# Decoder layer, feed-forward: the quantised activations turned by a DMA instead of by TensorE and VectorE

## The chip, the cores and the metric

The kernel runs on one core of one Trainium2 chip. The metric is the device time of one execution in microseconds (us). Three executions of the kernel before were timed, and one more was recorded by the hardware profiler. Times in rows of the trace count from the start of the profiled span.

## The reference, cut to what matters

The layer has three parts, each added to x: an attention, a long convolution, and a feed-forward part. Only the last is touched. It works on 2048 rows (8 sequences of 256) of 512 numbers, with ternary weights and activations rounded to whole numbers between -127 and 127:

```python
def activation_quant(x):
    scale = 127.0 / jnp.clip(jnp.max(jnp.abs(x), axis=-1, keepdims=True), EPS, None)
    return jnp.clip(jnp.round(x * scale), -128.0, 127.0) / scale
def bit_linear(x, w):                       # w: weight_quant(w), ternary
    return jnp.einsum('bsh,oh->bso', activation_quant(x), weight_quant(w))

gate = bit_linear(x, w_gate)                # 512 -> 2048
up = bit_linear(x, w_up)                    # 512 -> 2048
activated = up * jnp.square(jax.nn.relu(gate))
activated = subln(activated, subln_weight)  # by the row's mean square, times a weight
return bit_linear(activated, w_down)        # 2048 -> 512
```

The last `bit_linear` sums over the 2048 columns of `activated`. TensorE sums over partitions, so the rounded activations, which lie with a row of the batch in each partition, have to be turned so that a column lies in each partition. The change is to how they are turned.

## The kernel before, in words

The work is cut into NT = 16 tiles of 128 rows. Each of the five queues (SyncE, TensorE, ScalarE, VectorE, GpSimd) runs its own list of instructions in order, and they meet at semaphores. In the feed-forward part, `schedule` (L966) calls each engine's `turn(t, r, ...)` for t = 0 to 15, turns 4 to 13 in a loop of two (r = t mod 2, the buffer). The order inside a turn is written out by hand. A turn works on three or four tiles at once: it makes the activations of tile t, ends the quantisation of tile t-1, does the down projection of tile t-2, and prepares the rows of tile t+2.

A tile's 2048 columns go through in four chunks of 512 (n = 0 to 3):

- TensorE (L1057): for each chunk 4 matmuls for the gate and 4 for up (L1066). After chunk 0 it turns the convolution's output of tile t+2 (L1027); after chunk 1 it turns the rounded activations of tile t-2, 16 blocks of 128x128 bf16, into PSUM (`turn_act`, L1043); after chunk 2 it turns the rows of tile t+1 (L1035). At the end of the turn come the 16 matmuls of the down projection of tile t-2 (`down`, L1054). The matmuls of chunks 2 and 3 wait for VectorE's chunks 0 and 1 to free their PSUM banks.
- ScalarE (L1114): relu (L1093) and square (L1095) of each gate chunk; the sum of squares of each product (L1104); the copy of the turned rows (L1108); and, between the sums of chunks 2 and 3, the scaling of all of tile t-1 (`quantise`, L1112).
- VectorE (L1235): the product of each chunk (`chunk`, L1189), the largest of each chunk (`greatest`, L1193), the scales of tile t-1 (`scale`, `scale_b`, L1199 to L1219), the layer norm and rounding of tile t+2 (`rows_x2` L1138, `rows_stats` L1143, `rows_mean` L1148, `rows_norm` L1156, `rows_greatest` L1160, `rows_scale`, `rows_int` L1175 to L1179). It copies the turned activations of tile t-2 out of PSUM in two halves (`act_out`, L1225): half 0 just before `scale_b`, whose first instruction (L1211) waits for GpSimd's power r4 (L1314), and half 1 just after chunk 2. The last instruction of a turn is `final` (L1233), which ends tile t-2.
- GpSimd (L1326): the weighing of each chunk (`weigh`, L1318), two small powers (L1314), and at the end of the turn the rounding of tile t-1 to bf16 (`integers`, L1324) into act8.
- SyncE: DMAs of the convolution's output into `conv_part` for the tile to be turned (`place`, L986), and the stores of finished tiles (`store`, L994).

Turns 0 and 1 have no down projection (`last=False`), so in them neither `turn_act`, `act_out`, `down` nor `final` is issued. Turns 14 and 15 prepare no more rows (`rows=False`). Behind turn 15 come the scales of tile 15, its quantisation and rounding, and then `turn_act`, both `act_out`, `down`, `final` and the store of tiles 14 and 15, one after the other.

Of the kernel before, what the change touches and what calls it, by code (L numbers as in the profile page):

```python
# [31 lines left out]
P = 128  # L32
# [35 lines left out]
def wait(eng, signal, turn, n):  # L68
    eng.wait_ge(signal.sem, signal.at(turn, n))  # L69


def apart(eng):

    eng.nop(nofuse=True)
# [824 lines left out]
def ffn(nc, ctx, m, g, out, multiply, add_up):  # L899
# [5 lines left out]
    def sb(name, shape, dt=F32):  # L905
        return ctx.enter_context(nc.sbuf_tensor(name, shape, dt))

    def two(name, shape, dt=F32):
        return [sb(f"{name}{r}", shape, dt) for r in range(2)]

    def sig(name, per=1):
        return Signal(ctx.enter_context(nc.semaphore("f_" + name)), per)
# [23 lines left out]
    act_w = [m.big[:, 0:FF], m.big[:, FF:2 * FF]]  # L936
    act32 = m.big[:, 2 * FF:3 * FF]
    act8 = [y.bitcast(BF16)[:, 0:FF] for y in ys]
    act8t = sb("act8t", [P, FK, P], BF16)
    mb4 = sb("mb4", [P, IC])  # L940
    cc, sm, var, r4, cr, mb, bm, rb, qs = (sb(n, [P, 1]) for n in (
        "cc", "sm", "var", "r4", "cr", "mb", "bm", "rb", "qs"))
    fd = two("fd", [P, 1])
    ot = two("ot", [P, C])
    GB, UB, TB, NB, DB = m.ps[:, 0:2, :], m.ps[:, 2:4, :], m.ps[:, 4, :], m.ps[:, 5:7, :], m.ps[:, 7, :]
    tbb = TB.bitcast(BF16)

    first_banks, first_rows = [GB[:, 0, :], GB[:, 1, :]], UB[:, 0, :].bitcast(BF16)
    nbb = NB.rearrange("p a b -> p (a b)").bitcast(BF16)

    d_g, c_ident, c_half, c_w3 = (sig(n) for n in ("g_in", "ident", "half", "w3"))
    s_turned, s_x2, s_bn, s_mv, s_ve, s_rs, s_xn = (sig(n) for n in (
# [3 lines left out]
    s_g, s_u, s_rl, s_r2, s_a, s_as, s_w, s_mb4 = (sig(n, IC) for n in ("g", "u", "rl", "r2", "a", "as", "w", "mb4"))  # L956
    s_sm, s_cc, s_var, s_r4, s_mb, s_cr, s_bm, s_rb, s_qs, s_fd = (sig(n) for n in (
        "sm", "cc", "var", "r4", "mb", "cr", "bm", "rb", "qs", "fd"))
    s_a32, s_a8, s_a8t, s_dn, s_fin = (sig(n) for n in ("a32", "a8", "a8t", "dn", "fin"))
    s_a8e = sig("a8e", 2)  # L960
    d_place = sig("d_place", 16)
    d_o = [sig("d_o0"), sig("d_o1")]

# [19 lines left out]
    def sync(sp):  # L983

        def place(t, half=0):
            sp.dma_start(conv_part[:], qo[:, :, bass.ds(t * T - half * (B * T - P), P)]).then_inc(d_place.sem, 16)  # L986

        def place_next(t, half=0):
            wait(sp, s_turned, t - 1, 1)
            place(t, half)  # L990

        def store(t, r, half=0):
            wait(sp, s_fin, t, 1)
            sp.dma_start(outv[bass.ds(t * TT - half * (NT - 1), 1)].rearrange("o p c -> (o p) c"), ot[r][:]  # L994
                         ).then_inc(d_o[r].sem, 16)

        sp.wait_ge(m.s_red.sem, H2 // 2)
        place(2)
        sp.wait_ge(m.s_tern.sem, PIECES)
        sp.dma_start(gb[:], g.rearrange("(o n) -> o n", o=1).broadcast_to([P, FF])).then_inc(d_g.sem, 16)  # L1000
        place_next(3)
        place_next(4)
        for t in range(3):
            place_next(t + 5)
            store(t, t % 2)
        sp.wait_ge(m.s_red.sem, H2)
        place_next(B, 1)
        store(3, 1)
        with sp.Fori(2, 4) as i:
            for r in range(2):  # L1010
                place_next(2 * i + r + 5, 1)
                store(2 * i + r, r)
        for t in range(B, B + 3):
            place_next(t + 5, 1)
            store(t, t % 2, 1)
        for t in range(B + 3, NT):
            store(t, t % 2, 1)
        for r in range(2):
            sp.wait_ge(d_o[r].sem, 16 * NT // 2)

    def tensor(pe):
# [13 lines left out]
                mm = pe.transpose(bank[:, k * P:(k + 1) * P], xq[r][:, k * P:(k + 1) * P], identb[:])  # L1035
            mm.then_inc(s_xqt.sem, 1)

        def turn_act(t, r, first=False):
            wait(pe, s_a8, t, 1)
            if not first:  # L1040
                wait(pe, s_a8e, t - 1, 2)
            for k in range(FK):
                mm = pe.transpose(nbb[:, k * P:(k + 1) * P], act8[r][:, k * P:(k + 1) * P], identb[:])  # L1043
            mm.then_inc(s_a8t.sem, 1)

        def down(t, first=False):
            if first:
                pe.wait_ge(m.s_tern.sem, PIECES)
            else:
                wait(pe, s_fin, t - 1, 1)  # L1050
            for k in range(FK):
                if k % (FK // 2) == 0:
                    wait(pe, s_a8e, t, k // (FK // 2) + 1)
                mm = pe.matmul(DB, act8t[:, k, :], down_w[:, k, :], start=(k == 0), stop=(k == FK - 1))  # L1054
            mm.then_inc(s_dn.sem, 1)

        def turn(t, r, after=True, last=True, rows=True, more=True, stored=True, pair=None):  # L1057
            wait(pe, s_xqe, t, 1)
            for n in range(IC):
                if n >= 2:  # L1060
                    wait(pe, s_a, t, n - 1)
                elif after:
                    wait(pe, s_a, t - 1, n + 3)
                for bank, wt, s in ((GB, gate_w, s_g), (UB, up_w, s_u)):
                    for k in range(CK):
                        mm = pe.matmul(bank[:, n % 2, :], xqt[r][:, k, :], wt[:, k, n * C:(n + 1) * C],  # L1066
                                       start=(k == 0), stop=(k == CK - 1))
                    mm.then_inc(s.sem, 1)
                if n == 0 and rows:
                    turn_conv_part(t + 2)  # L1070
                if n == 1 and last:
                    turn_act(t - 2, r, first=not stored and r == 0)
                if n == 2 and more:
                    turn_rows(t + 1, 1 - r, behind=rows)
            if last:
                down(t - 2, first=not stored and r == 0)

        pe.wait_ge(m.s_red.sem, H2 // 2)
        pe.wait_ge(m.s_z1.sem, H2 - 1)
# [4 lines left out]
        pe.wait_ge(m.s_tern.sem, PIECES * 2 // 3)  # L1084
        schedule(turn, pe.Fori)
        for t in (NT - 2, NT - 1):
            turn_act(t, t % 2)
            down(t)

    def scalar(act):  # L1090
        def relu(t, n):
# [40 lines left out]
    def vector(dve):  # L1132
# [86 lines left out]
            nc.vector.tensor_scalar(fd[r][:], bm[:], m.wmean[:, 2:3], 1.0 / 127.0, ALU.mult, ALU.mult  # L1219
                                    ).then_inc(s_fd.sem, 1)  # L1220

        def act_out(t, h):
            wait(dve, s_a8t, t, 1)
            half_k, half_n = FK // 2, FF // 2
            nc.vector.tensor_copy(act8t[:, h * half_k:(h + 1) * half_k, :].rearrange("p k t -> p (k t)"),  # L1225
                                  nbb[:, h * half_n:(h + 1) * half_n]).then_inc(s_a8e.sem, 1)

        def final(t, r, stores):
            wait(dve, s_dn, t, 1)
            wait(dve, s_fd, t, 1)  # L1230
# [4 lines left out]
        def turn(t, r, after=True, last=True, rows=True, more=True, stored=True, pair=None):  # L1235
# [15 lines left out]
                scale(t - 1, 1 - r)  # L1251
            if rows:
                rows_mean(t + 2)
            if last:
                act_out(t - 2, 0)
            if after:
                scale_b(t - 1, 1 - r)
            if rows:
                rows_var(t + 2)
            greatest(t, 0, r)  # L1260
            chunk(t, 2)
            if last:
                act_out(t - 2, 1)
            greatest(t, 1, r)
            if rows:
                rows_norm(t + 2)
# [37 lines left out]
        scale(NT - 1, 1)  # L1304
        scale_b(NT - 1, 1)
        for t in (NT - 2, NT - 1):
            for h in range(2):
                act_out(t, h)
            final(t, t % 2, NT // 2 - 1)

    def gpsimd(pool):
# [6 lines left out]
            nc.gpsimd.tensor_tensor(act_w[r][:, n * C:(n + 1) * C], a[n % 2][:], gb[:, n * C:(n + 1) * C], ALU.mult  # L1318
                                    ).then_inc(s_w.sem, 1)

        def integers(t, r):
            wait(pool, s_a32, t, 1)
            apart(pool)
            nc.gpsimd.tensor_scalar(act8[r][:], act32, 1.0, -MAGIC, ALU.mult, ALU.add).then_inc(s_a8.sem, 1)  # L1324

        def turn(t, r, after=True, last=True, rows=True, more=True, stored=True, pair=None):  # L1326
            weigh(t, 0, r)
            if after:
                power(r4, var, s_var, s_r4, t - 1)
            weigh(t, 1, r)  # L1330
            if rows:
                power(rs, ve, s_ve, s_rs, t + 2)
            weigh(t, 2, r)
            weigh(t, 3, r)
            if after:
                integers(t - 1, 1 - r)

        nc.gpsimd.memset(identb[:], 0.0).then_inc(c_ident.sem, 1)
        pool.wait_ge(c_ident.sem, 1)
# [103 lines left out]
```

## Time and profile before

| what | value |
|---|---|
| median of 3 executions | 687.07 us (686.49 to 687.9) |
| profiled execution, its time | 686.38 us |
| profiled execution, its span | 684.6 us |
| mean granted TensorE clock over the span | 0.970 |
| TensorE matmul busy | 624.9 us, 91% |
| VectorE busy | 508.5 us, 74% |
| ScalarE busy | 455.5 us, 67% |
| GpSimd busy | 269.7 us, 39% |
| VectorE, L1225, the 32 copies that the change takes out | 656 to 691 ns each |
| GpSimd, L1324, the 16 roundings | 1890 to 1915 ns each |

The span runs from the first to the last instruction; the execution's own time is 1.8 us longer. The feed-forward part takes about the last 225 us: turn 1 starts on VectorE at 475.9 us, turn 14 at 648.7 us. Shares of busy time are means over parts that are limited by different engines, so a stretch has to be read by itself. "Releaser" of a wait is the instruction whose end came last by the trace.

### The profile page before, as it was taken

How to read it: one execution, taken by the hardware profiler on the slowest of the kernel's cores; microseconds unless marked ns; L12 is line 12 of the kernel's file. 1: busy time of each engine (PE TensorE's matmuls, PEld its weight loads, DVE VectorE, ACT ScalarE, POOL GpSimd, SP SyncE). 2: the span in 40 equal slices, each digit the busy share in tenths (PEclk: the TensorE clock that was granted, in tenths of full speed). 3: DMA queues.
4: the chain of work that ended last, by engine and by line, in shares of the span. 5: the costliest groups of instructions: out<-in, count | busy, mean ns of one | idle time of the engine just before them, and what ended most of it. 6: DMA issues, size and time to landing. Idle time of an engine off the chain costs nothing.

```text
span 684.6 us, 10990 instructions
## 1 busy us (share of the span) xinstructions
PE 624.9 (91%) x3074; PEld 355.3 (52%) x3074; DVE 508.5 (74%) x981; ACT 455.5 (67%) x799; POOL 269.7 (39%) x248
## 2 busy tenths in 40 slices
PE   5889999999999998989999999948799999999995
PEld 3535454545454543467777777723344444444442
DVE  3556757575847373547887788789999999999983
ACT  2354666676665746168889888845876777577691
POOL 1000010001010003057777777624665666566572
PEclk9969999999999997999999999978999999999999
DMA  8564153627180816045666556511011100100001
GB/s 316 140 182 93 31 124 123 148 97 191 55 240 17 234 37 153 11 145 162 168 192 173 173 164 193 156 70 31 17 32 48 45 31 31 61 31 31 31 17 46
DMA packets 42309, 72.51 MB, mean 106 GB/s; under 512 B 4720, under 2 KB 16496, under 8 KB 42160
## 3 DMA queue, kind: packets, MB, share of 16 engines
q1 hardware_dynamic: 42288, 72.26, 36.7%
q8 instruction: 10, 0.16, 0.1%
q14 instruction: 11, 0.09, 0.0%
HBM read 47.51 MB, written 4.28 MB: 76 GB/s over the span
## 4 chain that ended last, share of the span: by engine, by line
PE 26%; DVE 24%; issue 5%; DVEq 1%; ACT 1%; POOL 0%; ACTq 0%; POOLq 0%
PE ps L708 20%; DVE toep L1189 4%; DVE xq L1175 3%; PE ps L1066 3%; DVE mb L1193 3%; DVE act8t L1225 2%; PE ps L1054 2%; DVE mx L1160 1%; DVE x_all L1138 1%; DVE st L1143 1%; DVE xn L1156 1%; DVE qo L761 1%; DVEq L69 1%; DVE ot L1233 1%; DVE cx L1171 0%
## 5 line engine op out<-in xcount | busy, mean ns | idle before, releaser
L708 PE MATMUL ps<-kv,toep 128*128 128x288 f32 x640 | 157.1, 409 | 1.1 <-PEq L1378 1.1
L708 PEld LDWEIGHTS ps<-kv,toep 128*128 128x128 f32 x640 | 122.2, 191 | 36.0 <-issue 2.2
L1066 PE MATMUL ps<-wt,xqt 128*128 128x512 bf16 x512 | 123.8, 387 | 9.4 <-DVE toep L1189 8.5
L1318 POOL TENSOR_TENSOR big<-toep,wst 128x512 f32<-128x512 f32 x64 | 83.6, 1306 | 59.7 <-DVE toep L1189 59.7
L396 ACT ACTIVATE big<-ps,kscale 128x512 f32<-128x512 f32 x128 | 84.3, 695 | 14.1 <-PE ps L246 13.3
L246 PE MATMUL ps<-qx,kx 128*128 128x512 f32 x128 | 76.7, 634 | 12.4 <-ACT big L396 12.1
L1066 PEld LDWEIGHTS ps<-wt,xqt 128*128 128x128 bf16 x512 | 48.3, 99 | 67.1 <-DVE toep L1189 11.9
L761 DVE TENSOR_REDUCE qo<-big 128x2048 f32 (+1 forms) x32 | 72.2, 2257 | 0.0
L1104 ACT ACTIVATE asq<-toep 128x512 f32<-128x512 f32 x64 | 39.5, 618 | 44.7 <-DVE sm L1199 43.7
L696 POOL TENSOR_TENSOR kv<-ctx 128x768 f32<-128x768 f32 (+1 forms) x32 | 52.5, 1642 | 37.0 <-PE ps L708 28.2
L750 DVE TENSOR_TENSOR big<-ps,qd 128x1024 f32<-128x1024 f32 x32 | 39.2, 1225 | 37.0 <-ACT ys L840 34.4
L1054 PE MATMUL ps<-wt,act8t 128*128 128x512 bf16 x256 | 59.9, 379 | 7.3 <-DVE act8t L1225 7.3
L550 DVE RECIPROCAL yt<-ps 128x512 f32<-128x512 f32 x16 | 53.6, 3351 | 14.6 <-PE ps L264 14.6
L217 PE MATMUL ps<-wq_s,xt 128*128 128x512 f32 x128 | 63.3, 593 | 0.8 <-ACT xt L360 0.8
L800 POOL TENSOR_TENSOR big<-ys,qd 128x768 f32<-128x768 f32 x32 | 56.3, 1759 | 13.7 <-ACT ys L840 11.5
L284 PE MATMUL ps<-wo_s,yt 128*128 128x512 f32 x128 | 56.6, 594 | 1.0 <-DVE yt L555 1.0
L246 PEld LDWEIGHTS ps<-qx,kx 128*128 128x128 f32 x128 | 25.7, 205 | 46.4 <-ACT big L396 26.6
L646 POOL COPY vo<-vn 128x256 f32<-128x256 f32 x8 | 3.2, 397 | 111.7 <-PE ps L273 86.3
L1189 DVE TENSOR_TENSOR toep<-ps,kv 128x512 f32<-128x512 f32 x64 | 43.5, 680 | 3.8 <-ACT kv L1095 2.4
L1054 PEld LDWEIGHTS ps<-wt,act8t 128*128 128x128 bf16 x256 | 23.9, 98 | 40.4 <-DVE act8t L1225 11.0
L1093 ACT ACTIVATE kv<-ps 128x512 f32<-128x512 f32 x64 | 37.6, 587 | 10.6 <-PE ps L1066 10.6
L1193 DVE TENSOR_REDUCE mb<-big 128x1 f32<-128x512 f32 x64 | 43.3, 677 | 0.0
(121 smaller groups left out, 1018.5 us busy)
## 6 DMA issues: line engine op xcount, KB each, us to landing
qx<-kv SPq DMA_DIRECT2D x128, 128.0 KB, 2.4
wst<-in_wall SPq DMA_DIRECT2D x12, 1024.0 KB, 6.8
wst<-in_wall SPq DMA_DIRECT2D x48, 256.0 KB, 3.8
toep<-krows SPq DMA_DIRECT2D x32, 256.0 KB, 3.7
ctx<-in_ctxt SPq DMA_DIRECT2D x32, 192.0 KB, 2.6
out_y<-ot SPq DMA_DIRECT2D x16, 256.0 KB, 2.0
conv_part<-qo SPq DMA_DIRECT2D x14, 256.0 KB, 2.7
x_all<-in_x SPq DMA_DIRECT2D x2, 1536.0 KB, 14.4
```

Source lines behind the costliest of these rows:

```text
L217: mm = pe.matmul(bank[:, t, :], xt[:, k, t * P:(t + 1) * P], wq_s[:, k, :], start=(k == 0), stop=(k == CK - 1))
L246: pe.matmul(SB[:, n % 2, :], kx[:, kv, s * P:(s + 1) * P].bitcast(F32R), qx[:, kv, gp * C:(gp + 1) * C].bitcast(F32R), start=True, stop=Tr ...
L284: mm = pe.matmul(OB[:, t, :], yt[:, k, t * P:(t + 1) * P], wo_s[:, k, :], start=(k == 0), stop=(k == CK - 1))
L396: act.activation(pt[:, s, kv, gp * C:(gp + 1) * C], SB[:, n % 2, :], ACT.Exp, scale=kscale[:, c:c + 1]).then_inc(s_e.sem, 1)
L708: mm = pe.matmul(m.ps[:, LB * r + lb, :].rearrange("p (b s) -> p b s", s=WIDE)[:, :, 0:PAIRS], m.toep[r][:, d * P:(d + 1) * P], m.kv[r][:, ...
L761: nc.vector.tensor_reduce(qo[:, :, bass.ds(h * HD, HD)], z[r][:], AX.X, ALU.add).then_inc(s_red.sem, 1)
L800: nc.gpsimd.tensor_tensor(z[r][:, :, :, HD - SHIFTS:HD].rearrange("p n j s -> p n s j"), window(ys[r][:], SHIFTS - 1, (SHIFTS * EW, NB), ( ...
L1054: mm = pe.matmul(DB, act8t[:, k, :], down_w[:, k, :], start=(k == 0), stop=(k == FK - 1))
L1066: mm = pe.matmul(bank[:, n % 2, :], xqt[r][:, k, :], wt[:, k, n * C:(n + 1) * C], start=(k == 0), stop=(k == CK - 1))
L1189: nc.vector.tensor_tensor(a[n % 2][:], UB[:, n % 2, :], r2[n % 2][:], ALU.mult).then_inc(s_a.sem, 1)
L1193: nc.vector.tensor_reduce(mb4[:, n:n + 1], act_w[r][:, n * C:(n + 1) * C], AX.X, ALU.max, apply_absolute_value=True).then_inc(s_mb4.sem, 1)
L1318: nc.gpsimd.tensor_tensor(act_w[r][:, n * C:(n + 1) * C], a[n % 2][:], gb[:, n * C:(n + 1) * C], ALU.mult).then_inc(s_w.sem, 1)
```

## The change

`turn_act` of TensorE and `act_out` of VectorE are taken out. SyncE gets a `turn_act`: it waits for GpSimd's rounding of the tile and issues one DMA that reads act8 (128 partitions by 2048 bf16, 512 KB) and writes it turned into act8t (128 by 16 by 128). act8t is held twice, one buffer for even and one for odd tiles. TensorE's `down` waits for this DMA. GpSimd's `integers` of tile t newly waits for the down projection of tile t-2, which shows that the DMA has read act8's buffer. The PSUM banks that held the turned activations are no longer used.

```diff
-    act8t = sb("act8t", [P, FK, P], BF16)
+    act8t = two("act8t", [P, FK, P], BF16)
...
+        def turn_act(t, r):
+            wait(sp, s_a8, t, 1)
+            apart(sp)
+            sp.dma_start(act8t[r][:], act8[r], transpose=True).then_inc(d_a8t[r].sem, 16)
...
         place_next(4)
+        turn_act(0, 0)
         for t in range(3):
             place_next(t + 5)
+            turn_act(t + 1, (t + 1) % 2)
             store(t, t % 2)
         sp.wait_ge(m.s_red.sem, H2)
         place_next(B, 1)
+        turn_act(4, 0)
         store(3, 1)
         with sp.Fori(2, 4) as i:
             for r in range(2):
                 place_next(2 * i + r + 5, 1)
+                turn_act(2 * i + r + 1, 1 - r)
                 store(2 * i + r, r)
         for t in range(B, B + 3):
             place_next(t + 5, 1)
+            turn_act(t + 1, (t + 1) % 2)
             store(t, t % 2, 1)
-        for t in range(B + 3, NT):
+        for t in range(B + 3, NT - 1):
+            turn_act(t + 1, (t + 1) % 2)
             store(t, t % 2, 1)
+        store(NT - 1, 1, 1)
...
-        def turn_act(t, r, first=False):
-            wait(pe, s_a8, t, 1)
-            if not first:
-                wait(pe, s_a8e, t - 1, 2)
-            for k in range(FK):
-                mm = pe.transpose(nbb[:, k * P:(k + 1) * P], act8[r][:, k * P:(k + 1) * P], identb[:])
-            mm.then_inc(s_a8t.sem, 1)
-
-        def down(t, first=False):
+        def down(t, r, turned, first=False):
+            pe.wait_ge(d_a8t[r].sem, turned * 16)
             if first:
                 pe.wait_ge(m.s_tern.sem, PIECES)
             else:
                 wait(pe, s_fin, t - 1, 1)
             for k in range(FK):
-                if k % (FK // 2) == 0:
-                    wait(pe, s_a8e, t, k // (FK // 2) + 1)
-                mm = pe.matmul(DB, act8t[:, k, :], down_w[:, k, :], start=(k == 0), stop=(k == FK - 1))
+                mm = pe.matmul(DB, act8t[r][:, k, :], down_w[:, k, :], start=(k == 0), stop=(k == FK - 1))
...
-                if n == 1 and last:
-                    turn_act(t - 2, r, first=not stored and r == 0)
...
         for t in (NT - 2, NT - 1):
-            turn_act(t, t % 2)
-            down(t)
+            down(t, t % 2, NT // 2)
...
-        def act_out(t, h):
-            wait(dve, s_a8t, t, 1)
-            half_k, half_n = FK // 2, FF // 2
-            nc.vector.tensor_copy(act8t[:, h * half_k:(h + 1) * half_k, :].rearrange("p k t -> p (k t)"),
-                                  nbb[:, h * half_n:(h + 1) * half_n]).then_inc(s_a8e.sem, 1)
...
-            if last:
-                act_out(t - 2, 0)
             if after:
                 scale_b(t - 1, 1 - r)
...
             chunk(t, 2)
-            if last:
-                act_out(t - 2, 1)
             greatest(t, 1, r)
...
         for t in (NT - 2, NT - 1):
-            for h in range(2):
-                act_out(t, h)
             final(t, t % 2, NT // 2 - 1)
...
-        def integers(t, r):
+        def integers(t, r, after=True):
             wait(pool, s_a32, t, 1)
+            if after:
+                wait(pool, s_dn, t - 2, 1)
             apart(pool)
```

## Rows read from the trace of the kernel before

**Rows 1.** Windows of a middle turn and of turn 1: length, busy by engine, clock, DMA.

```profile
core 0: us, PE busy (x) PEld busy (x) DVE busy (x) ACT busy (x) POOL busy (x), PEclk, DMA share, GB/s
581.99:595.33 13.34, 12.42 (x75) 6.19 (x73) 13.06 (x35) 9.59 (x19) 8.14 (x7) 1.00 0.12 39
475.86:488.55 12.69, 9.28 (x54) 4.32 (x53) 11.90 (x32) 10.31 (x20) 8.14 (x7) 1.00 0.15 43
```

**Rows 2.** Timeline of the middle turn: start, us, engine, line, operation, [idle before <-releaser].

```profile
581.99 0.68 DVE L1189 TENSOR_TENSOR toep<-ps,kv 128x512 f32<-128x512 f32 x1
...
585.55 0.66 DVE L1225 COPY act8t<-ps 128x1024 bf16<-128x1024 bf16 x1
585.56 0.55 POOL L1314 TENSOR_TENSOR r<-var,fhalf 128x1 f32<-128x1 f32 x1 [1.51 <-DVE var L1204]
...
586.14 0.21 DVE L1211 TENSOR_SCALAR cr<-r,cf_all 128x1 f32<-128x1 f32 x1
...
587.82 0.68 DVE L1189 TENSOR_TENSOR toep<-ps,kv 128x512 f32<-128x512 f32 x1
...
588.41 0.68 DVE L1225 COPY act8t<-ps 128x1024 bf16<-128x1024 bf16 x1
588.58 1.30 POOL L1318 TENSOR_TENSOR big<-toep,wst 128x512 f32<-128x512 f32 x1 [0.64 <-DVE toep L1189]
...
589.61 0.56 DVE L1156 TENSOR_SCALAR xn<-x_all,mv,rs 128x512 f32 x1
...
590.08 0.68 DVE L1189 TENSOR_TENSOR toep<-ps,kv 128x512 f32<-128x512 f32 x1
```

**Rows 3.** Timeline of turn 1, which has no L1225.

```profile
475.86 0.68 DVE L1189 TENSOR_TENSOR toep<-ps,kv 128x512 f32<-128x512 f32 x1
...
479.44 0.55 POOL L1314 TENSOR_TENSOR r<-var,fhalf 128x1 f32<-128x1 f32 x1 [1.52 <-DVE var L1204]
...
480.02 0.21 DVE L1211 TENSOR_SCALAR cr<-r,cf_all 128x1 f32<-128x1 f32 x1 [0.51 <-POOL r L1314]
...
482.45 1.29 POOL L1318 TENSOR_TENSOR big<-toep,wst 128x512 f32<-128x512 f32 x1 [0.64 <-DVE toep L1189]
...
482.88 1.15 DVE L1156 TENSOR_SCALAR xn<-x_all,mv,rs 128x512 f32<-128x512 f32 x1
...
483.95 0.68 DVE L1189 TENSOR_TENSOR toep<-ps,kv 128x512 f32<-128x512 f32 x1
```

**Rows 4.** DMA issues: transfer, count, KB each, median us from issue to landing.

```profile
out_y<-ot SPq DMA_DIRECT2D x16, 256.0 KB, 2.0
conv_part<-qo SPq DMA_DIRECT2D x14, 256.0 KB, 2.7
...
wst<-in_g SPq DMA_DIRECT2D x1, 1024.0 KB, 4.6
```

**Rows 5.** Timeline, from one middle turn's chunk 0 on TensorE to the next down projection.

```profile
590.89 1.89 PE L1066 MATMUL ps<-wt,xqt 128*128 128x512 bf16 x8
...
592.11 1.90 POOL L1324 TENSOR_SCALAR ys<-big 128x2048 bf16<-128x2048 f32 x1
...
593.07 0.63 ACT L1095 ACTIVATE kv<-kv 128x512 f32<-128x512 f32 x1
...
600.18 1.89 PE L1054 MATMUL ps<-wt,act8t 128*128 128x512 bf16 x8
```

**Rows 6.** Timeline of the end: tiles 13 and 15.

```profile
657.61 1.90 POOL L1324 TENSOR_SCALAR ys<-big 128x2048 bf16<-128x2048 f32 x1 [0.49 <-ACT big L1112]
...
664.37 3.62 PE L1054 MATMUL ps<-wt,act8t 128*128 128x512 bf16 x16
...
668.02 0.75 DVE L1233 SCALAR_TENSOR_TENSOR ot<-ps,fd,x_all 128x512 f32<-128x512 f32 x1 [0.91 <-PE ps L1054]
...
673.73 1.90 POOL L1324 TENSOR_SCALAR ys<-big 128x2048 bf16<-128x2048 f32 x1 [3.30 <-ACT big L1112]
...
677.69 3.61 PE L1054 MATMUL ps<-wt,act8t 128*128 128x512 bf16 x16 [0.87 <-DVE act8t L1225]
```

**Rows 7.** Window after TensorE's idle stretch before turn 0: length, PE busy, clock, DMA.

```profile
457.00:462.40 5.40, 4.63 (x16) 0.50 0.05 21
```

More of the change, by code:

```diff
@@ L944, in ffn @@
     ot = two("ot", [P, C])
-    GB, UB, TB, NB, DB = m.ps[:, 0:2, :], m.ps[:, 2:4, :], m.ps[:, 4, :], m.ps[:, 5:7, :], m.ps[:, 7, :]
+    GB, UB, TB, DB = m.ps[:, 0:2, :], m.ps[:, 2:4, :], m.ps[:, 4, :], m.ps[:, 7, :]
     tbb = TB.bitcast(BF16)
     first_banks, first_rows = [GB[:, 0, :], GB[:, 1, :]], UB[:, 0, :].bitcast(BF16)
-    nbb = NB.rearrange("p a b -> p (a b)").bitcast(BF16)
     d_g, c_ident, c_half, c_w3 = (sig(n) for n in ("g_in", "ident", "half", "w3"))
@@ L958, in ffn @@
         "sm", "cc", "var", "r4", "mb", "cr", "bm", "rb", "qs", "fd"))
-    s_a32, s_a8, s_a8t, s_dn, s_fin = (sig(n) for n in ("a32", "a8", "a8t", "dn", "fin"))
-    s_a8e = sig("a8e", 2)
+    s_a32, s_a8, s_dn, s_fin = (sig(n) for n in ("a32", "a8", "dn", "fin"))
+    d_a8t = [sig("d_a8t0"), sig("d_a8t1")]
     d_place = sig("d_place", 16)
@@ L1075, in turn @@
             if last:
-                down(t - 2, first=not stored and r == 0)
+                down(t - 2, r, pair if stored else 1, first=not stored and r == 0)
         pe.wait_ge(m.s_red.sem, H2 // 2)
@@ L1335, in turn @@
             if after:
-                integers(t - 1, 1 - r)
+                integers(t - 1, 1 - r, after=last and (stored or r == 1))
         nc.gpsimd.memset(identb[:], 0.0).then_inc(c_ident.sem, 1)
```

## The prediction

> **What bounds the kernel now.** The change touches only the feed-forward turns, so I read stretches, not the page's totals. First the windows of one turn in the middle: 13.34 us long, VectorE busy 13.06 us of it and TensorE 12.42 us [rows 1]. Both look full, and a reader would subtract here: two copies less on VectorE, 16 block transposes less on TensorE, a shorter turn. The window cannot say that; it counts an instruction as busy also where it is held up. So I next put two timelines side by side: the middle turn [rows 2], and turn 1, which has no down projection yet and so neither copy [rows 3]. Turn 1 is a trial of the change's effect on VectorE that the kernel before already holds. From its first product (chunk 0) to L1211, the first instruction that needs GpSimd's power, the middle turn takes 586.14 - 581.99 = 4.15 us and turn 1 480.02 - 475.86 = 4.16 us. From L1211 to chunk 3 it is 590.08 - 586.14 = 3.94 us with the copy and 483.95 - 480.02 = 3.93 us without. Turn 1 is 12.69 us against 13.34 [rows 1], and the 0.65 us between them is `final`, which turn 1 lacks too (0.75 us a piece [rows 6], each instruction starting a little before the end of the one before). The two copies lie in time that VectorE would otherwise wait out.
>
> **Part 1, the copies (L1225).** Half 0 runs 585.55 to 586.21 beside GpSimd's power, which starts at 585.56 and ends at 586.11; L1211 starts at 586.14 [rows 2]. Without the copy L1211 waits for the same power: in turn 1 it stood idle 0.51 us, released by L1314 [rows 3]. Worth nothing. The cover is the power and the scales before it, and those stay. Half 1 starts at 588.41 and pushes what follows by 0.60 us, so that L1156 starts at 589.61 and takes 0.56 us. GpSimd's weighing L1318 runs from 588.58 to 589.88 [rows 2]. Without the copy L1156 would start at 589.01, inside that. In turn 1 it does: it starts at 482.88 while L1318 runs from 482.45 to 483.74, and takes 1.15 us instead of 0.56, to end 0.29 us behind L1318's end [rows 3]; in the middle turn it ends at 590.17, also 0.29 us behind L1318's end. So half 1 is worth nothing either: VectorE is held up by GpSimd instead. Sum for the 12 turns 2 to 13: 0 us, with 0.59 us each (7.1 us) as the other bound of one half, 14.2 us of both. I take 0, because turn 1 measures it.
>
> **Part 2, the transposes on TensorE (L1043).** They stand between chunk 1 and chunk 2. Chunk 2's matmuls wait for VectorE's chunk 0, chunk 3's for its chunk 1, and VectorE's order is unmoved by part 1. TensorE idles a little more; nothing on the path gets earlier. 0 us. At the end, turn 15 has less to do on VectorE and TensorE, but tile 13's down projection will wait for its DMA there (part 4), so I take 0 again; the bound below is -0.6 us, the place of one copy on VectorE.
>
> **Part 3, the DMA.** No row shows a transposing DMA. What is needed is L, from the end of the rounding to the turned tile in SBUF. SyncE is idle when the rounding ends (the store of the tile before waits for `final`, later; the placing has been issued a turn ago), so L is issue to landing. By bytes: 256 KB land in 2.0 us and 1024 KB in 4.6 us [rows 4], so 512 KB in about 2.9 us. That is the lower bound. By pieces: `conv_part` has the bytes of `out_y` in 512 pieces (4 rows of 512 B for each partition) instead of 128 and takes 0.7 us longer [rows 4], 1.8 ns for each piece more. A turned 128x128 block of bf16 has rows of 256 B, 2048 of them in the tile: 2.9 + 1920 x 1.8 ns = 6.4 us. The upper bound is everything by pieces, four times `conv_part`: 10.8 us. I take 6.4 us, since the cost of pieces is measured on a copy inside SBUF like this one. The trace shows no transfer at all in which data are turned, so nothing here tells how much slower or not that is. The Trainium skill, Advanced Engine Details and Errata, section on the X-bar transpose, says that such a DMA is as fast as a regular one; by it L would be the 2.9 us of the byte rows.
>
> Is L covered in a middle turn? The rounding ends at 592.11 + 1.90 = 594.01 and the down projection of that tile starts at 600.18 [rows 5]: 6.17 us. If it starts later, the next chunk 0 on TensorE is late, then its relu and square, then VectorE's chunk 0. From that chunk 0 on TensorE (590.89) to the end of its square (593.07 + 0.63) are 2.81 us [rows 5]; VectorE takes the product at 595.33, the end of the window [rows 1], 1.6 us later. TensorE also loses 0.42 us in `down` now, waiting for half 1, which goes. So L up to 8.2 us costs a middle turn nothing. Beyond that the loop is: VectorE's chunk 0 to the rounding's end 594.01 - 581.99 = 12.02, then L, then `down` 3.62 [rows 6], then 2.81, over two turns: 18.45 + L against 2 x 13.34 = 26.68. With L = 6.4: 0 us. SyncE's stores and placings come behind the transpose in its queue by its issue time; they are needed a turn later and cost nothing. GpSimd's new wait, `integers` on the down projection two tiles back, is met by then (that projection ended before 590.89, the rounding starts at 592.11 [rows 5]), and only the next turn's weighing stands behind it. 0 us.
>
> **Part 4, the end.** Here the cover is gone. Tile 13 is rounded at 657.61 + 1.90 = 659.51; its down projection started at 664.37 [rows 6], 4.86 us later, and now starts L later. `final` of tile 13 (668.02) follows it, and on VectorE the last largest value and all scales of tile 15 stand behind `final`; the rounding of tile 15 (673.73) follows these. First term: L - 4.86. Then tile 15 is rounded at 675.63 and was projected at 677.69 [rows 6]: 2.06 us for transposes, copies and all. Second term: L - 2.06. With L = 6.4: 1.5 + 4.3 = 5.9 us. Only the store is behind it, as before. TensorE's clock: after its idle stretch before turn 0 the window shows a granted clock of 0.50, that is 1.2 GHz, for about 5 us [rows 7]. At the end TensorE now idles for over 5 us between the projections of tiles 13 and 14. At the upper level a matmul of `down` takes 3.62 / 16 = 0.23 us [rows 6]; at half the clock half of tile 14's 16 would cost some 1.8 us more, but the wait for tile 15's own DMA covers most of that. I take 0, bound +1.8.
>
> **The sum:** 0 + 0 + 0 + 5.9 = +5.9 us on the profiled execution (686.38 us; its span 684.6 and 1.8 around it), which stands 0.7 us below the median of 687.07. I add it to the median: 693.0 us. A measurement of this kernel can tell about 0.2% (1.4 us) from no change.
>
> **The rivals.**
>
> *A, the forecast, 46%.* L between 4.1 and 8.2 us: only the end pays, twice. The first term starts from 0 at L = 4.86, so +2.0 to +9.5 us: 689 to 696.6 us.
>
> *B, the DMA is quick, 15%.* L from 2.9 to 4.1 us, the byte rows. Then the first term is 0 or a little below and the second 0.8 to 2.0: 687.3 to 689 us, mostly within 0.2%. Against it: the pieces of 256 B. The skill's rule named above is this case.
>
> *C, late by pieces, 22%.* L over 8.2 us, up to the 10.8 of the rows and somewhat past. At 10.8 two turns take 29.25 us instead of 26.68, +2.6 us for each of 6 pairs = 15.4 us, and the end 2 x 10.8 - 6.92 = 14.7 us: 717 us. VectorE would then wait at chunk 0 (L1189) for ScalarE or TensorE every turn, where it has no idle time now. For it: cost by pieces, unknown cost of turning. Against: pieces overlapped well in `conv_part`.
>
> *D, faster, 10%.* The place is VectorE between chunk 2 and chunk 3 and at L1211. If L1156 were not held up by L1318 but ran in 0.56 us, and the power came earlier, turns 2 to 13 would each lose 1.19 us: -14.2 + 5.9 = -8.3, 678.8 us. Half 1 alone gives 7.1 us, -1.2 net, the point from which it decides. For it: VectorE is 98% busy by the window, and it loses two instructions. Against it: turn 1.
>
> *E, block by block, 7%.* The DMA turns 16 blocks of 128x128 one after the other. If each cost as much as the shortest row, 2.0 us [rows 4], L is 32 us, two turns take 50.5 us, +23.8 for each pair = 143, and the end +57: 887 us. The Trainium skill, Vector Engine: DVE Perf Modes, section on the three transpose paths, gives 1309 ns for a 128x128 block by DMA; by it, an estimate, 16 blocks in series are 21 us and the kernel near 800 us.
>
> **How the numbers follow.** The likeliest is A, at 693.0 us. 686.5 to 718 us holds A, B and 19 of the 22% of C; D and E and the rest of C, 20%, lie outside. A's own range is 689 to 697. Faster by over 0.2%: D, 10%. Within 0.2%: most of B, 14%. Slower: 76%.
>
> **What would show it.** The turns of the loop still 13.3 us; no L1225 and no L1043; L1211 idle 0.5 us before it, released by L1314, in every turn; L1156 at 1.15 us in all middle turns; the transposing DMA near 6.4 us to landing; TensorE waiting for DMA at L1054 for tiles 13, 14 and 15, and not before; the span from `final` of tile 13 to the end longer by 4.3 us. The forecast is wrong if the middle turn changes: shorter means D, longer with VectorE idle before chunk 0 means C or E. If the turn holds and the total is off, L was.

## The result, and the profile after

| | before | after |
|---|---|---|
| median | 686.58 us (6 executions) | 691.36 us (6 executions, 690.06 to 692.86) |
| ratio | | 1.0070, 95% interval 1.0053 to 1.0088 |
| span of the profiled execution | 684.6 us | 689.0 us |
| VectorE's chunk 0 of turn 0 | at 461.9 us | at 460.9 us |

The change costs 4.8 us; 5.9 were forecast. What comes ahead of the feed-forward part is untouched, but the start of turn 0 lies anywhere from 460.9 to 464.1 us in the profiled executions of the kernels shown here, one execution each. So from here on I compare stretches between the starts of chunk 0 on VectorE, each from one profiled execution, and set totals beside them.

First the middle turn, as in [rows 1]. It is 13.40 us long; TensorE has 1.05 us less to do and VectorE 0.45 us less, and neither shortens the turn:

```profile
581.40:594.80 13.40, 11.37 (x56) 5.32 (x56) 12.61 (x33) 9.48 (x18) 8.17 (x7) 1.00 0.33 78
```

The timeline of this turn shows why. It answers to [rows 2], line numbers moved by one (L1210 for L1211, L1155 for L1156, L1188 for L1189):

```profile
581.40 0.68 DVE L1188 TENSOR_TENSOR toep<-ps,kv 128x512 f32<-128x512 f32 x1
...
584.98 0.55 POOL L1301 TENSOR_TENSOR r<-var,fhalf 128x1 f32<-128x1 f32 x1 [1.51 <-DVE var L1203]
...
585.56 0.21 DVE L1210 TENSOR_SCALAR cr<-r,cf_all 128x1 f32<-128x1 f32 x1 [0.51 <-POOL r L1301]
...
587.99 1.31 POOL L1305 TENSOR_TENSOR big<-toep,wst 128x512 f32<-128x512 f32 x1 [0.64 <-DVE toep L1188]
...
588.42 1.16 DVE L1155 TENSOR_SCALAR xn<-x_all,mv,rs 128x512 f32 x1
...
589.50 0.68 DVE L1188 TENSOR_TENSOR toep<-ps,kv 128x512 f32<-128x512 f32 x1
```

L1210 now stands idle 0.51 us for GpSimd's power, where the first copy ran. L1155 takes 1.16 us instead of 0.56: it starts while GpSimd's weighing holds it up and ends 0.28 us behind that. Both are turn 1 of the kernel before [rows 3], to 0.01 us. Of the 1.34 us that the two copies took, nothing comes back.

The DMA, from issue to landing, as the last part of the profile's page has it:

```profile
act8t<-ys SPq DMA_TRANSPOSE x16, 4.3
```

4.3 us, against 6.4 forecast; a tile's down projection in a middle turn starts when it did.

The end, answering to [rows 6]:

```profile
668.40 0.75 DVE L1226 SCALAR_TENSOR_TENSOR ot<-ps,fd,x_all 128x512 f32<-128x512 f32 x1 [0.29 <-PE ps L1056]
...
674.94 1.90 POOL L1313 TENSOR_SCALAR ys<-big 128x2048 bf16<-128x2048 f32 x1 [3.33 <-ACT big L1111]
...
675.50 5.68 PE L1056 MATMUL ps<-wt,act8t 128*128 128x512 bf16 x16 [7.13 <-DMA act8t<-ys]
...
681.21 0.75 DVE L1226 SCALAR_TENSOR_TENSOR ot<-ps,fd,x_all 128x512 f32<-128x512 f32 x1 [8.46 <-PE ps L1056]
...
682.11 3.61 PE L1056 MATMUL ps<-wt,act8t 128*128 128x512 bf16 x16 [0.94 <-DVE ot L1226]
```

Tile 15 is rounded at 676.84 and projected at 682.11, 5.27 us later instead of 2.06. TensorE waited 7.13 us for tile 14's DMA, and then did that tile's 16 matmuls in 5.68 us instead of 3.62. The `final` of tile 14 came late by this, and tile 15's projection waited for it, 0.94 us beyond its own DMA. From the start of tile 13's `final` to the end of the span are 20.6 us instead of 16.6: 4.0 more, where 4.3 were forecast.

A place that the forecast did not have is in turn 14: chunk 2's 8 matmuls take 3.50 us, where they took 1.90. The windows of 3.5 us from there (PE busy, clock, DMA), first after, then the same place before:

```profile
649.09:652.59 3.50, 3.50 (x11) 0.53 0.79 185
```

```profile
649.43:652.93 3.50, 3.50 (x20) 1.00 0.19 75
```

The granted clock is 0.53 there, close to its lower level (1.2 GHz). TensorE had stood idle for 2.21 us, where in the kernel before the block transposes ran.

The same happens once more in the changed kernel, in turn 2, and there it costs nothing:

```profile
488.50 3.58 PE L1068 MATMUL ps<-wt,xqt 128*128 128x512 bf16 x8 [2.69 <-DVE toep L1188]
```

The granted clock over turn 2 is 0.87, as it is over turn 14 (0.86); before, both had 1.00. But turn 2 takes 13.34 us as before, because VectorE, and not TensorE, sets its pace. In turn 14, which has no rows to prepare and is 2.8 us shorter, TensorE's loss shows.

The account of the 5.4 us from chunk 0 of turn 0 to the end (before 222.7 us, after 228.1):

| stretch | before | after | difference |
|---|---|---|---|
| turns 0 and 1 | 26.67 | 26.86 | +0.2 |
| turns 2 to 13, each | 13.345 | 13.383 | +0.04, x12 = +0.5 |
| turn 14 | 10.55 | 11.83 | +1.3 |
| from chunk 0 of turn 15 | 25.36 | 28.81 | +3.4 |

The 0.2 us of turns 0 and 1 say little: in the kernels shown here this stretch takes 26.45 to 26.90 us.

### The profile page after: what moved, and what is told of

It is laid out like the page before. It is cut to its first block, busy times and chain, and to the rows that moved or that the text cites. A ratio compares the mean times of both kernels' runs of the same rounds, so it can differ in the third digit from the quotient of the medians.

```text
span 689.0 us, 10465 instructions
## 1 busy us (share of the span) xinstructions
PE 613.6 (89%) x2818; PEld 341.5 (50%) x2818; DVE 498.1 (72%) x949; ACT 455.0 (66%) x799; POOL 270.0 (39%) x248
## 4 chain that ended last, share of the span: by engine, by line
PE 25%; DVE 19%; issue 6%; POOL 3%; ACT 2%; DVEq 1%; DMA 1%; ACTq 0%; POOLq 0%; SPq 0%
PE ps L708 20%; DVE xq L1174 3%; DVE toep L1188 3%; PE ps L1068 3%; DVE mb L1192 3%; DVE xn L1155 2%; POOL big L1305 2%; PE ps L1056 2%; DVE mx L1159 1%; DVE qo L761 1%; POOL r L1301 1%; DMA act8t<-ys 1%; DVE ot L1226 1%; DVEq L69 0%; DVE cx L1170 0%
## 5 line engine op out<-in xcount | busy, mean ns | idle before, releaser
L1068 PE MATMUL ps<-wt,xqt 128*128 128x512 bf16 x512 | 126.9, 395 | 28.8 <-DVE toep L1188 28.0
L396 ACT ACTIVATE big<-ps,kscale 128x512 f32<-128x512 f32 x128 | 84.9, 695 | 13.7 <-PE ps L246 12.0
L800 POOL TENSOR_TENSOR big<-ys,qd 128x768 f32<-128x768 f32 x32 | 56.3, 1760 | 13.7 <-ACT ys L840 11.6
L1188 DVE TENSOR_TENSOR toep<-ps,kv 128x512 f32<-128x512 f32 x64 | 43.4, 679 | 4.8 <-ACT kv L1094 3.5
L1056 PEld LDWEIGHTS ps<-wt,act8t 128*128 128x128 bf16 x256 | 25.4, 100 | 40.3 <-DMA act8t<-ys 9.0
```

Of the source, the lines that this page charges most:

```text
L396: act.activation(pt[:, s, kv, gp * C:(gp + 1) * C], SB[:, n % 2, :], ACT.Exp, scale=kscale[:, c:c + 1]).then_inc(s_e.sem, 1)
L800: nc.gpsimd.tensor_tensor(z[r][:, :, :, HD - SHIFTS:HD].rearrange("p n j s -> p n s j"), window(ys[r][:], SHIFTS - 1, (SHIFTS * EW, NB), ( ...
L1056: mm = pe.matmul(DB, act8t[r][:, k, :], down_w[:, k, :], start=(k == 0), stop=(k == FK - 1))
L1188: nc.vector.tensor_tensor(a[n % 2][:], UB[:, n % 2, :], r2[n % 2][:], ALU.mult).then_inc(s_a.sem, 1)
```

## The experiments

**1. The block transposes back on TensorE, for nothing (warm).** They run where they did, also ahead of the last two down projections, and write PSUM that nobody reads; the DMA still feeds `down`.

```diff
+        def keep_warm(t, r):
+            wait(pe, s_a8, t, 1)
+            for k in range(FK):
+                pe.transpose(nbb[:, k * P:(k + 1) * P], act8[r][:, k * P:(k + 1) * P], identb[:])
...
+                if n == 1 and last:
+                    keep_warm(t - 2, r)
...
         for t in (NT - 2, NT - 1):
+            keep_warm(t, t % 2)
             down(t, t % 2, NT // 2)
```

> The changed kernel with TensorE's 16 block transposes of the old kernel put back at their old places, into PSUM banks that nobody reads (added work, the DMA still feeds the down projection). Theory 1 (the missing transposes let TensorE's clock fall at a few places: chunk 2 of turn 14 takes 3.50 us for 8 matmuls instead of 1.90, tile 14's down projection 5.68 instead of 3.62): both are back at 1.9 and 3.6 us, the kernel is 1.5 to 2.2 us faster than the changed one, about 689.3 us, although it does more work. Rival (the clock falls because of the waits for the DMA at the end alone): turn 14 is back, tile 14's down projection still takes over 5 us, and only 1.3 us return. Rival 2 (TensorE's work is on the path): slower than the changed kernel by up to 0.5 us a turn. The middle turn stays at 13.3 to 13.4 us in theory 1.

Median 691.04 us, ratio to before 1.0056 (1.0036 to 1.0077). Against the changed kernel's 691.36 us the executions show no gain. In the profiled one the start of turn 0 was at 463.6 us, 2.7 us later than in the changed kernel's; whether the edit itself moves that start was not tried. By stretches: turns 13.386 us, turn 14 10.55 (after: 11.83), from turn 15 on 27.94 (28.81); from turn 0, 225.6 against 228.1. Turn 14 is fully back, by added work. Tile 14's projection still takes 5.15 us: theory 1 is half wrong, the first rival holds for that place. That TensorE's work is on the path of the turn is refuted: the turns hold with the transposes in.

```profile
651.45 1.90 PE L1074 MATMUL ps<-wt,xqt 128*128 128x512 bf16 x8 [0.93 <-DVE toep L1197]
...
676.25 5.15 PE L1062 MATMUL ps<-wt,act8t 128*128 128x512 bf16 x16 [3.27 <-DMA act8t<-ys]
```

**2. Tiles 14 and 15 turned as before, the rest by DMA (tail).**

```diff
         for t in (NT - 2, NT - 1):
-            down(t, t % 2, NT // 2)
+            end_act(t, t % 2)
+            end_down(t, t % 2)
...
         for t in (NT - 2, NT - 1):
+            for h in range(2):
+                end_out(t, h)
             final(t, t % 2, NT // 2 - 1)
```

`end_act` is the 16 transposes into PSUM, `end_out` one of VectorE's two copies out of it, `end_down` the 16 matmuls behind them; SyncE issues no DMA for these two tiles.

> The changed kernel, but the last two tiles (14 and 15), whose turning nothing covers, are turned as before, by TensorE and VectorE's copies; tiles 0 to 13 by the DMA. Theory (the loss sits in the uncovered DMA waits of the last two tiles, 2.4 us, and in the clock that falls while TensorE waits there, 0.8 us): 3 to 3.5 us faster than the changed kernel, 688 us, ratio to the kernel before about 1.002, what is left being the slower chunk 2 of turn 14 (1.3 us). Rival (the loss is spread over the loop, contention of the 512 KB transfers with all engines): the end gives back under 1 us and the total stays above 690.

Median 689.75 us (ratio 1.0029, 1.0006 to 1.0052). The end: 26.99 us, 1.8 us back; turn 14 stays at 11.87. Less than the 3 us expected, since tile 14's projection still ran at a lowered clock, 4.98 us, though nothing waited for a DMA there. That is the profiled execution, the slowest of 12. Four of the 12 took 686.3 to 686.9 us at a mean granted clock of 0.967 or 0.968, as fast as the kernel before; the other eight took 689.3 to 692.5 us at 0.962 to 0.965, the profiled one among them (0.962). So the same kernel loses the clock in one execution and seems to keep it in another, and the stretches of one execution do not tell how often.

**3. Both (tail_warm).**

> The changed kernel with both earlier repairs: tiles 14 and 15 turned by TensorE and VectorE, and in the turns TensorE's 16 block transposes put back for nothing. Measured apart, from chunk 0 of turn 0 to the end: 222.7 us in the kernel before, 228.1 in the changed one, 225.6 with the transposes back, 226.3 with the end back. Theory (the loss is the uncovered DMA at the end and TensorE's lower clock in turn 14 and at tile 14's down projection, and nothing else): together 223.2 us or less, the 0.5 us left being the 12 turns at 13.38 instead of 13.34 us; ratio to the kernel before 1.000 to 1.003. Rival (something in the loop or in SyncE's queue costs as well): over 224.5 us.

Median 687.27 us, ratio 0.9991 (0.9973 to 1.0008). Turn 14 10.55, end 25.35, from turn 0 223.26 us; tile 14's projection is at 3.61 us:

```profile
673.12 3.61 PE L1070 MATMUL ps<-wt,act8t 128*128 128x512 bf16 x16 [1.36 <-DVE act8t L1251]
```

All 12 executions had a mean granted clock of 0.969 or 0.970. The two repairs together bring back all but 0.5 us, and this 0.5 is the 12 turns at 13.386 instead of 13.345. Here VectorE does only 4 of the 32 copies and TensorE all of the transposes: 28 copies less are worth nothing in this order of instructions.

**4. The copy's worth in another order (order_after, order_before).** In both kernels VectorE does the largest value of chunk 0 ahead of the scales, and the norm directly behind chunk 2.

```diff
             if after:
+                wait(dve, s_mb, t - 1, 1)
+            greatest(t, 0, r)
+            if after:
                 scale_b(t - 1, 1 - r)
             if rows:
                 rows_var(t + 2)
-            greatest(t, 0, r)
             chunk(t, 2)
-            greatest(t, 1, r)
             if rows:
                 rows_norm(t + 2)
+            greatest(t, 1, r)
```

In the kernel before, the norm also goes ahead of the second copy.

> The changed kernel with two instructions of VectorE moved: the largest value of chunk 0 goes ahead of the scales (into the wait for GpSimd's power), the layer norm of the next rows goes directly behind chunk 2 (ahead of GpSimd's weighing of chunk 2). Theory (the two copies that were taken out are worth 0.51 and 0.6 us a turn, hidden by two stalls: L1210 waiting for the power and the norm held up by the weighing): with the stalls filled the middle turn drops from 13.4 to 12.3 to 12.5 us, 12 turns bring 11 to 13 us, about 679 us, faster than both kernels. If only one stall goes, 12.9 us and 685 us. Rival (TensorE or ScalarE bounds the turn at 13.3 us as well): the turn stays above 13.2 us and the total within 1 us of 691.

> The kernel before, with the same two moves on VectorE and the two copies kept. Theory (in the kernel before both stalls were already filled, by the copies): the moves bring nothing, middle turn 13.2 to 13.4 us, total within 1.4 us of 686.6. Rival (the order alone is better, whatever the copies do): the turn falls as in the changed kernel with the moves, to 12.5 us, and the total to 675 us.

Both forecasts missed, and the pair says more than either. The changed kernel: 691.21 us (ratio 1.0068, 1.0045 to 1.0091), turn 13.34 us, no gain. The kernel before: 702.32 us (ratio 1.0220, 1.0195 to 1.0245), turn 14.58 us. In the same order the two copies cost 14.58 - 13.34 = 1.24 us a turn. The first stall was filled (L1210 waits no longer). The second grew, as the rows of the changed kernel in this order show:

```profile
586.85 1.68 DVE L1155 TENSOR_SCALAR xn<-x_all,mv,rs 128x512 f32 x1
...
586.95 1.30 POOL L1307 TENSOR_TENSOR big<-toep,wst 128x512 f32<-128x512 f32 x1
```

By the record the norm starts 0.10 us ahead of the weighing and still loses: it ends 0.28 us behind it. So it goes in 10 of the 12 turns (1.58 to 1.68 us). In turns 5 and 7 the norm went first and took 0.54 and 0.55 us, once with the same lead of 0.10 us. These two turns took 13.02 us, and not the 12.3 to 12.5 expected, for VectorE now met the next of GpSimd's instructions, the rounding (L1315, 538.23 to 540.20):

```profile
538.49 2.00 DVE L1178 TENSOR_SCALAR xq<-xq 128x512 bf16<-128x512 f32 x1
```

This took 0.42 us in the other ten. So what the first stall gave, the second took, and behind the second stands a third; with the copies in, nothing hides them any more. This bears out the reading of turn 1: the copies are real work that was free only where they stood.

**5. The DMA as a plain copy (plain),** which leaves the turning out, so that the down projection gets unturned activations.

```diff
-            sp.dma_start(act8t[r][:], act8[r], transpose=True).then_inc(d_a8t[r].sem, 16)
+            sp.dma_start(act8t[r].rearrange("p k t -> p (k t)"), act8[r]).then_inc(d_a8t[r].sem, 16)
```

> The changed kernel with the DMA of the activations as a plain copy of the same 512 KB between the same buffers (128 rows of 4 KB each, nothing is turned, so the down projection gets the activations unturned). It measures the cost of turning. Theory 1 (turning costs by its 256 B pieces or by the turning itself): the plain copy lands in about 2.9 us, against 4.3 us, its issue takes 0.3 to 0.4 us against 1.8. Rival (a transposing DMA is as fast as a regular one): the plain copy takes 4.0 to 4.3 us as well.

```profile
L999 SPq DMA_DIRECT2D act8t<-ys x16: 470/494/501, 488.8 to 678.8; - x16
...
DMA to landing us min/median/max: 2.9/2.9/3.3
```

Theory 1 holds. Issue 0.49 us (after: 1.80), landing 2.9 us (4.3). Turning costs 1.4 us of latency and 1.3 us of SyncE. Whether it does so by its 256 B pieces or by the turning itself, the plain copy, which has neither, cannot tell. The middle turn is 13.39 us here too: the DMA's cost inside is covered, whatever its form. Total 692.09 us in one execution, from turn 0 227.5 us, 0.6 less than the changed kernel, because the end waits 1.4 us less for a DMA but pays more of it to the clock (tile 14's projection 6.07 us).

**6. Three transposing DMAs for one (three_dma):** two more into free memory, ahead of the real one. SyncE waits in addition for the three of the tile before, which had landed long since in the rows below.

```diff
...
+                sp.wait_ge(d_a8t[1 - r].sem, before * 48)
             apart(sp)
+            for n in range(2):
+                sp.dma_start(spare[n], act8[r], transpose=True).then_inc(d_a8t[r].sem, 16)
             sp.dma_start(act8t[r][:], act8[r], transpose=True).then_inc(d_a8t[r].sem, 16)
...
-            pe.wait_ge(d_a8t[r].sem, turned * 16)
+            pe.wait_ge(d_a8t[r].sem, turned * 48)
```

> The changed kernel with two more transposing DMAs of the same tile, into memory that nobody reads, ahead of the real one; the down projection waits for all three (added work: 1 MB more to move for each tile). From rounding to landing 4.3 us become about 4.3 + 2 x 1.8 = 8 us, if the DMAs follow one another at the pace of the issues. Theory (up to 8.2 us are covered in a middle turn): the turn stays at 13.4 to 13.5 us, and what is lost lies behind chunk 0 of turn 14, 2 x 3.7 us or somewhat more. Rival (the cover is only the 6.2 us to the down projection, as TensorE has no slack behind it): each turn grows by about (8 - 6.2) = 1.8 us or half of that, 10 to 20 us for the loop. If the landing comes out at 9 us or more the theory says (18.45 + L) / 2 for a turn.

712.80 us in one execution. The issues took longer than I had taken, 2.3 us each; a middle turn of this kernel, from the rounding to `down`'s next wait:

```profile
586.56 1.90 POOL L1321 TENSOR_SCALAR ys<-big 128x2048 bf16<-128x2048 f32 x1
...
588.63 4.64 SPq L1006 DMA_TRANSPOSE big<-ys  x2
...
593.32 2.34 SPq L1007 DMA_TRANSPOSE act8t<-ys  x1
...
597.92 2.33 PE L1064 MATMUL ps<-wt,act8t 128*128 128x512 bf16 x10 [2.38 <-DMA act8t<-ys]
```

Rounded at 588.46, projected at 597.92: L = 9.5 us. The formula says (18.45 + 9.5) / 2 = 13.97 us for a turn; the mean of the 12 is 14.15. Ten of them lie between 13.4 and 14.2 us; turns 2 and 4 took 16.2 and 16.6 us, which the formula does not explain. TensorE's clock has a part in them: the granted clock was 0.79 and 0.90 over these two and 1.00 over the other ten, and the down projection, 3.62 us elsewhere, took 5.02 and 5.31 us in them. L was 9.4 to 10.4 us over the 12 turns, 9.7 in the mean, which gives 14.06. The rival (every microsecond beyond 6.2 counts, in full or by half) would give 16.7 or 15.0 us for a turn, and ten of the twelve lie well under both: there is slack behind the down projection.

**7. An order that uses the time (norm_final), and the same with the copies (norm_final_before).** The norm goes directly ahead of chunk 2; `final` goes ahead of the rounding on VectorE.

```diff
+            if after:
+                wait(dve, s_mb, t - 1, 1)
+            greatest(t, 0, r)
             if after:
                 scale_b(t - 1, 1 - r)
             if rows:
                 rows_var(t + 2)
-            greatest(t, 0, r)
+            if rows:
+                rows_norm(t + 2)
             chunk(t, 2)
             greatest(t, 1, r)
-            if rows:
-                rows_norm(t + 2)
             chunk(t, 3)
...
-            if rows:
-                rows_int(t + 2, r)
             if last:
                 final(t - 2, r, pair - 1 if stored else None)
+            if rows:
+                rows_int(t + 2, r)
```

> The changed kernel with three moves on VectorE: the largest value of chunk 0 ahead of the scales; the layer norm directly ahead of chunk 2, where GpSimd cannot start a weighing (it waits for chunk 2); the final of tile t-2 ahead of the rounding of tile t+2, into the time in which GpSimd's rounding holds VectorE's up. Theory (VectorE's turn is its instructions plus what GpSimd holds up, and TensorE and ScalarE have over 1 us to spare): the norm takes 0.5 to 0.6 us instead of 1.15 to 1.7, the held part of the rounding shrinks from 1.1 to 0.5 us, the turn drops from 13.4 to 12.5 to 13.0 us, 5 to 10 us less in all, 681 to 686 us. Rival (something else, ScalarE's chain or the down projection, bounds the turn at 13.3 us): no change, 691 us.

> The kernel before with the same three moves, copies kept. Theory (with VectorE's stalls filled otherwise, the two copies cost their 0.6 us each): the turn is 1.1 to 1.3 us longer than that of the changed kernel with the same moves, 13.7 to 14.2 us, total 690 to 697. Rival (the copies are free in any order): the same turn as there.

The changed kernel in this order: 684.48 us, ratio to the kernel before 0.9962 (0.9947 to 0.9978), turn 12.88 us. The kernel before in this order: 690.29 us, ratio 1.0045 (1.0023 to 1.0067), turn 13.61 us; a little under the 13.7 to 14.2 expected, and the difference of the two is under the 1.1 to 1.3 expected. The norm runs free now, since GpSimd has nothing that it could start before chunk 2:

```profile
584.63 0.55 DVE L1155 TENSOR_SCALAR xn<-x_all,mv,rs 128x512 f32 x1 [0.67 <-POOL rs L1303]
```

The rounding of the rows (L1174) is still held up, though: it takes about 1.48 us here, 1.72 in the changed kernel, 0.48 where nothing holds it up; less of that went than expected. The copies cost 13.61 - 12.88 = 0.73 us a turn in this order, between the 0 of the given order and the 1.24 of experiment 4.

**8. The version that beats both (best_tail), and with the spare transposes (best_tail_warm).** Experiment 7's order with experiment 2's end; then also experiment 1.

> The changed kernel with the three moves on VectorE that brought its turn from 13.38 to 12.88 us, and with tiles 14 and 15 turned by TensorE and VectorE as before. Theory: the stretch behind chunk 0 of turn 15 falls from 29.1 to about 27 us as it did alone (28.8 to 27.0), so 1.8 to 2.5 us less, 682.3 us in all, ratio to the kernel before 0.993. Rival (with the shorter turns the end is bound otherwise, by ScalarE): no gain over 684.5 us.

> The same as the kernel before it in this call, with the 16 block transposes back in TensorE's turns for nothing. Theory (they hold the clock at its upper level at the end, and TensorE has the time): 0.5 to 1.5 us less again, 681 us. Rival (with turns of 12.9 us TensorE's time is on the path): 1 to 5 us more, turns of 13.0 us and over.

best_tail: 682.22 us, ratio 0.9927 (0.9902 to 0.9952), turn 12.89, end 25.28 us: 5.4 us under the 687.64 us of the kernel before in the same series, and the theory held. best_tail_warm: 682.36 us (0.9928, 0.9903 to 0.9952), turns 12.89, but an end of 27.03 us, where tile 14's projection took 5.24 us at a lowered clock in spite of the transposes; in best_tail it took 3.61 without them. In the medians neither the gain of the theory nor the loss of the rival came. The two profiled executions differ by 2.2 us from chunk 0 of turn 0 to the end (219.1 against 216.9), which turn 0's earlier start (460.9 against 462.9) hides in the total; since the medians agree, I lay nothing on that difference.

## Why the prediction was right

*Parts 1 and 2, the loop is worth nothing: right, and shown.* The rows after repeat turn 1 of before [rows 3]. Experiment 3 takes 28 copies away and stands at the old time; experiment 4 shows the same copies at 1.24 us a turn once the order is another. What was not foreseen is +0.04 us a turn: L1174, the rounding of the rows, takes 1.70 to 1.74 us in turns 4 to 13 instead of 1.67. It ends 0.28 us behind GpSimd's rounding before and after, and that rounding starts 0.03 to 0.07 us later there, 10.16 to 10.19 us behind chunk 0 instead of 10.12 to 10.13. The change gave it a new wait, for the down projection two tiles back, and part 3 put that at 0 us. The shift is in experiments 1 to 3 and 5 alike, so it is neither TensorE's idling nor the turning. That the wait itself is the cause is likely, but no run takes it out.

*Part 3, L: the size was off.* Taken 6.4 us, measured 4.3, which is only just inside the 4.1 to 8.2 us of rival A. The number of pieces was right: the page counts 38000 packets under 512 B after and 4720 before, some 2080 a tile. So was the base, the plain copy's 2.9 us. Laid on the pieces alone, the price of one was 1.4 us / 1920 = 0.7 ns, not the 1.8 ns taken from `conv_part`. That 1.8 ns came from comparing `conv_part`, a copy inside SBUF, with `out_y`, a store to HBM, so its 0.7 us need not be the pieces' alone. The Trainium skill's rule, that a transposing DMA is as fast as a regular one (Advanced Engine Details and Errata, X-bar transpose), does not hold for this size: 4.3 us against 2.9 in experiment 5. The Trainium skill's 1309 ns for a 128x128 block of bf16 by DMA (VectorE: DVE Perf Modes, The three transpose paths), taken 16 times in series, would be 21 us, an estimate; the 16 blocks landed in 4.3, so rival E is out. Experiment 6 bears out the loop's formula roughly: 13.97 us by the L of one turn, 14.06 by the mean L, against a mean of 14.15 over the twelve turns, and of 13.71 over the ten without the two odd ones.

*Part 4, the end: the sum right, its terms shifted.* The first term was L - 4.86; with L = 4.3 it is 0, and `final` of tile 13 came 0.6 us earlier after chunk 0 of turn 15 (8.21 us against 8.78), as turn 15 does two copies less, the bound I had named. But tile 15's power then queued behind GpSimd's rounding of tile 14, and the rounding of tile 15 began 6.54 us behind this `final` instead of 5.71: +0.8. The second term, L - 2.06, is 2.2 us for the DMA and 0.9 for the late `final` of tile 14, 3.2 in all, where 4.3 were forecast.

*The clock: the step that failed behind the right number.* Taken as 0. I had bounded it at 1.8 us at the end and covered it by tile 15's DMA. It cost 0.9 us there in spite of that, and 1.3 us in turn 14, where I had not looked: part 2 says "TensorE idles a little more", and priced only the time, not what idling does. The DMA's terms were 5.9 us where the trace has 2.2; the clock's 2.2, the loop's 0.5, the order at the end's 0.3 and 0.2 in turns 0 and 1 were not in the sum. The two errors, 3.7 too much and 3.2 too little, nearly cancel, and that is why 693.0 stands so near 691.4. The nearness is luck; what was foreseen is that the loop gives nothing and that the loss lies at the end.

What of the clock stays open: at turns of 13.4 us, turn 14 was slow in the four kernels without the transposes (after, tail, plain and order_after, 11.83 to 11.92 us, TensorE idle for 2.21 to 2.26 us ahead of chunk 2), and fast in the two with them (10.55 us, idle for 0.93); at turns of 12.9 us it was fast without them as well (10.56 us, idle for 1.57). In turn 2 the granted clock was 0.87 in these four and in norm_final, and 1.00 in the three with spare transposes, but also in best_tail, which has none. So the transposes were the cure in turn 14, as far as one profiled execution of each kernel shows. Tile 14's projection ran low in the changed kernel and seven of the experiments, with and without transposes (4.98 to 6.07 us), and at 3.61 us in tail_warm, best_tail and the three kernels with the copies in. The executions of tail at 0.967 show besides that the fall need not come each time. The rule by which idle stretches become a lower clock is not settled by these runs.

## What to carry to other kernels

A busy share of 98% on the engine that sets the pace does not price an instruction on it: look at what its neighbours wait for, and find a turn of the same kernel in which the instruction is missing. Work that fills a stall is free only where it stands; taking it out pays when the order is made anew around the hole, and then 0.7 to 1.2 us a turn came out of the same two copies. A latency that is covered in every turn of a loop has to be priced once more for the last turns, where nothing is left to cover it, and where the engine that waits may also lose its clock.

## What the runs showed of the hardware that was not expected

- A transposing DMA of 512 KB inside SBUF, bf16, 128 by 2048, in this kernel: 4.3 us from issue to landing and 1.8 us on the issuing queue; a plain copy of the same bytes 2.9 and 0.49 us.
- Between VectorE's norm (128x512 f32 from SBUF to SBUF) and GpSimd's product, the record's earlier start does not say who goes first: in experiment 4 the norm's record began 0.10 us ahead of the product's in two turns, and it took 1.68 us in one and 0.55 us in the other. What kept it free in every turn was to stand where GpSimd had nothing to start (experiment 7).
- 1 us of transposes less per turn left TensorE idle for 2.2 us at a stretch in turn 14, and the granted clock was then 0.53 for 3.5 us; with 16 transposes that nobody reads, the full clock was there in that place in both profiled executions. In turn 2 the same fall (3.58 us for 8 matmuls instead of 1.90) cost no time.
